# Moving the copy of dt\*x and renaming GpSimd's four input products in a fused attention and state-space kernel

## The chip, the cores and the metric

The kernel runs on one core of a Trainium2 chip. The metric is device microseconds of one execution, as the median of several. Engines are named TensorE (PE), VectorE (DVE), ScalarE (ACT), GpSimd (POOL) and SyncE (SP, which only issues DMAs).

## The reference

Input `x` is (8, 512, 64, 64) in float32: 8 images, 512 channels, 4096 positions. Layer 0 adds a pooled attention; layer 1, which holds nearly all the time, adds this:

```
xn = layer_norm(group_norm(x))                   # over the 512 channels
for each of 4 chunks of 128 channels, per image: # mamba
    xi, z = in_proj(chunk)                       # 256 inner channels each
    xc = silu(causal_conv(xi, 4 taps));  dt, B, C = x_proj(xc)
    dt = softplus(dt_proj(dt) + b)
    for s in range(16):                          # 16 states
        h_s[t] = exp(dt[t] * A_s) * h_s[t-1] + (dt*xc)[t] * B_s[t]
        y[t]  += h_s[t] * C_s[t]
    y = (y + xc * D) * silu(z);  chunk_out = out_proj(y) + skip * chunk
x = x + proj(layer_norm(all chunk_outs))
```

## The kernel before, in words

An image has 8 tiles of 512 positions, a tile has 4 items (the chunks), so there are 8 x 8 x 4 = 256 items. An item holds 256 inner channels as 128 partitions x 2 halves x 512 positions, and is worked off in 16 steps, one for each state s. Here "first" to "fourth item" of a tile are those with `j` = 0, 1, 2, 3 in the code. Each step does the following for its state:

- the **input product** U_s = (dt\*x) \* B_s, 1024 elements per partition. `make_u` stands both on VectorE (L1119) and on GpSimd (L1440); `POOL_U` (L43) names the four states that GpSimd makes, VectorE makes the other twelve. VectorE reads dt\*x from PSUM (`DTP`), GpSimd reads it from SBUF (`DTX`), and B_s is in SBUF;
- the **decay** exp(dt \* A_s) by ScalarE into PSUM (`DA`, `step`, L770), half by half. There is one buffer for each half, so that the decay of step s+1 waits for the scan of the same half of step s;
- the **scan** h_s, two instructions of VectorE (`scan`, L1140), one for each half;
- the **output product** G_s = h_s \* C_s on GpSimd (`out_state`, L1452);
- the **sum** of G_s into PSUM (`YP`) by TensorE with a unit matrix (`state_sum`, L390), issued two steps later in TensorE's order.

U, H and G are rings of 4 slots: the scan of state n waits for the output product n-4, an input product n waits for the scan n-4, and an output product n for the sum n-4.

All engines run their instructions in the order that the code writes, and the front of the next item is interleaved with the steps of this one. Where it stands in the steps (plus one step later in the fourth item, `d` = 1 from `late`, L202):

- TensorE: xi of the next item, first half, at step 15 of the item before (in the third item's case at step 0 of the fourth), second half (`xi_second`) at step 0 + d, ahead of the state sum 15 of the finished item, which is at step 1 (for d = 1 the order is sum 14, xi first half, sum 15, xi second half); z at step 2 + d.
- ScalarE: `xi_copy` at steps 1 + d and 2 + d, the two silus at step 3 + d (they wait for the gate), the softplus of dt at steps 6 to 10. In the fourth item two pieces of `apply_norm` follow the copy of the second half of xi at step 3.
- GpSimd: four products at steps 9 + d to 11 + d that finish dt; the last, `dt_x` (L1478), is dt\*x of the next item. Here its end is called **X** of the next item.
- VectorE: the **gate** (`gate`, L1154) of the finished item after the scan of step 2 + d. It waits for the state sum 15 of that item.
- `dtx_copy` (L843) on ScalarE copies dt\*x from SBUF into PSUM, since VectorE's input products read it there. In the kernel before it stands at step 13 + d of the item before, behind the decay of that step and ahead of the decay of the next; it waits for `dt_x` and for all of VectorE's input products of the item whose dt\*x it overwrites.

The tables `AHEAD` and `AHEAD_LATE` (L47, L48; the second for d = 1) say which input products VectorE issues ahead of the scan of each step; 16 is state 0 of the next item. GpSimd issues its input product of step n+3 ahead of the output product of step n (`U_LEAD`).

SyncE broadcasts two rows of B or of C by one DMA, in the order of the steps.

Of the kernel before, what the change touches and what calls it, by code (L numbers as in the profile page):

```python
# [22 lines left out]
NS = 16  # L23
# [16 lines left out]
B_ROWS = 8  # L40
C_ROWS = 4
SLICE_COLS = T // SS
POOL_U = (1, 7, 8, 10)  # L43
NP_U = len(POOL_U)
ND_U = NS - NP_U
U_LEAD = 3
AHEAD = ((2,), (3,), (), (4,), (5, 6,), (), (), (9,), (), (11,), (12,), (13,), (14,), (15,), (), (16,))  # L47
AHEAD_LATE = ((2,), (3,), (), (4,), (5,), (6,), (), (9,), (), (11,), (12,), (13,), (14,), (15,), (), (16,))  # L48


def block_ssm_kernel(nc, x, wqkv, bq, bk, bv, norm_g, norm_b, w_in, conv_w, conv_b, w_x, w_dt, dt_b,
                     a_log, d_param, w_out, w_proj, proj_b, skip, eye, group_mean, out):
    with ExitStack() as ctx:  # L53
# [128 lines left out]
        def pool_u(n):  # L182

            return n // NS * NP_U + sum(1 for s in POOL_U if s <= n % NS)

# [583 lines left out]
        def _(act):  # L769
# [73 lines left out]
            def dtx_copy(tile, i, first=False):  # L843
                act.wait_ge(dtx_ready, tile * ITEMS + i + 1)
                if not first:
                    act.wait_ge(u_dve, tile * (ND_U * ITEMS) + ND_U * i)
                act.activation(DTP[:, :, :], DTX[:, :, :], ACT.Copy).then_inc(dtx_copied, 1)  # L847
# [36 lines left out]
            def window(tile, w, first=False, front=True, ln1=True, ln2=True, new=False, shifted=False, coming=None, kept=True,  # L884
                       kept_before=True):
                j = w % ITEMS
                d = late(j, new)
                ahead = tile + w // ITEMS
                for s in range(NS):
                    step(tile, w * NS + s, first=first, kept=kept if s else kept_before)  # L890
                    if front:
                        if s == 1 + d:
                            xi_copy(tile, w + 1, 0)
                        if s == 2 + d:
                            xi_copy(tile, w + 1, 1)
                        if s == 3 + d:
                            if not first:
                                act.wait_ge(yz_ready, tile * ITEMS + w)
                            silus(tile, w + 1)
                        if s == 5 + d:  # L900
                            rows_copy(tile, w + 1)
                        if s == 6 + d:
                            dt_split(tile, w + 1, 0)
                        if s == 7 + d:
                            dt_split(tile, w + 1, 1)
                            dt_exp(tile, w + 1)
                        if s == 8 + d:
                            dt_excess(tile, w + 1)
                            dt_log(tile, w + 1)
                        if s == 9 + d:  # L910
                            dt_large(tile, w + 1)
                            dt_small(tile, w + 1)
                        if s == 10 + d:
                            dt_square(tile, w + 1, first=first)
                        if s == 12:
                            if j == 0 and ln2:
                                act.wait_ge(cen2_ready, ahead)
                            skip_term(tile, w + 1)
                        if s == 13 + d:
                            dtx_copy(tile, w + 1)  # L920
                    if j == 0 and ln2 and s == 11:
                        square(cen2_ready, sq2_ready, ahead)
                    if j == 0 and ln2 and s == 15:
                        rstd(RS[:, :], var2_ready, log2_ready, rstd2_ready, ahead)
                    if j == 2 and ln1:
                        if s == 4 + d:
                            act.wait_ge(x1_ready, ahead + 2)
                            if new:
                                act.wait_ge(gshift_ready, coming * 2 + 2)
                            group_norm((0, 1))  # L930
                        if s == 5 + d:
                            group_norm((2, 3), last=True)
                        if s == 9 + d:
                            square(cen1_ready, sq1_ready, ahead + 2)
                        if s == 13 + d:
                            rstd(LP[:, :], var1_ready, log1_ready, rstd1_ready, ahead + 2)
                        if s == 15 and not new:
                            keep_halo()
                            apply_norm(ahead + 2, (0,))
                    if j == 3 and ln1:  # L940
                        if s == 0:
                            if shifted:
                                keep_halo(new=True)
                                apply_norm(ahead + 2, (0,))
                            apply_norm(ahead + 2, (1,))
                        if s == 3:
                            apply_norm(ahead + 2, (2, 3))

                    if coming is not None:
                        if j == 1:  # L950
                            if s == 0:
                                prob_scale(coming)
                            if s == 9:
                                prob_turned(coming)
                            if s == 11:
                                attended(coming, 0)
                            if s == 13:
                                attended(coming, 1)
                        if j == 2 and not new:
                            if s == 14:  # L960
                                group_rstd(coming, 1)
                        if j == 2 and new and s == 1:
                            group_rstd(coming, 2)
                        if j == 3:
                            if s == 2:
                                pooled(coming)
                            if s == 7:
                                summed(coming)
                            if s == 11:
                                head(Q, BQ, q_ps, q_ready, coming, 0)  # L970
                            if s == 12:
                                head(Q, BQ, q_ps, q_ready, coming, 1)
                            if s == 13:
                                head(K, BK, k_ps, k_ready, coming, 0)
                            if s == 15:
                                head(K, BK, k_ps, k_ready, coming, 1)
                        if j == 0:
                            if s == 0:
                                value_copy(coming, 0)
                            if s == 10:  # L980
                                value_copy(coming, 1)
                            if s == 14:
                                prob(coming)
# [134 lines left out]
        def _(dve):  # L1118
            def make_u(tile, n, first=False):  # L1119
                i, s = n // NS, n % NS  # L1120
                if s not in POOL_U:
                    if s == min(set(range(NS)) - set(POOL_U)):
                        dve.wait_ge(dtx_copied, tile * ITEMS + i + 1)
                    if s % 2 == 0 or s - 1 in POOL_U:
                        q = s // 2
                        dve.wait_ge(b_landed[q % (B_ROWS // 2)],
                                    tile * rows_count(ITEMS - 1, NS // 2 - 1, B_ROWS // 2) + rows_count(i, q, B_ROWS // 2))
                    if not (first and n < used(n)):
                        dve.wait_ge(scanned, tile * (2 * STEPS) + 2 * (n - used(n) + 1))
                    dve.tensor_tensor(U[:, slot(n)], DTP[:, :, :], BS[:, s % B_ROWS, :].unsqueeze(1).broadcast_to([P, NH, T]),  # L1130
                                      ALU.mult).then_inc(u_dve, 1)

            def make_ahead(tile, n, d, first=False, front=True):

                s = n % NS
                for m in (AHEAD_LATE if d else AHEAD)[s]:
                    if front or m < NS:
                        make_u(tile, n - s + m, first=first)

            def scan(tile, n, first=False):  # L1140
                i, s = n // NS, n % NS
# [61 lines left out]
            def window(tile, w, stat=None, first=False, front=True, ln1=True, ln2=True, new=False, coming=None):  # L1203

                j = w % ITEMS
                d = late(j, new)
                ahead = tile + w // ITEMS
                for s in range(NS):
                    n = w * NS + s
                    make_ahead(tile, n, d, first=first, front=front)  # L1210
                    scan(tile, n, first=first)
                    if s == 2 + d and not first:
                        gate(tile, w - 1)
# [197 lines left out]

            attention()
            first_front(0, 0)
            make_u(0, 0, first=True)
            window(0, 0, first=True, ln2=False)
            window(0, 1, ln2=False)
            with dve.Fori(0, BATCH - 1) as b:
# [169 lines left out]
```

## Time and profile before

| | |
|---|---|
| median of 3 runs | 16507.46 us (16484.04 to 16516.45) |
| the profiled execution | 16491.02 us, its span 16489.2 us |
| GpSimd busy | 14793.6 us, 90% |
| VectorE busy | 14790.3 us, 90% |
| TensorE busy | 14324.9 us, 87% |
| ScalarE busy | 11509.3 us, 70% |

The span is that of the instructions in the hardware's record; the execution's own time is 1.8 us longer. A busy share is an average over all stages. "Idle before" is time that an engine spent idle in front of an instruction, with the instruction that released it.

### The profile page before, as it was taken

What the parts mean: (1) busy time and instruction counts of PE and PEld (TensorE: products, weight loads), DVE (VectorE), ACT (ScalarE), POOL (GpSimd) and SP (SyncE); (2) the same over time, 40 slices, a digit from 0 to 9 for tenths busy, and PEclk for the clock granted to TensorE, in tenths of its full rate; (3) what the DMA queues carried; (4) which work ended last, traced back from release to release, by engine and by line L of the source; (5) the groups of instructions that cost most, each with busy time, mean ns of one, the idle gap of its engine ahead of it and who ended that gap; (6) DMA issues with size and microseconds to landing.
All of it is one profiled execution on the core that took longest, in us unless ns stands there. A gap on an engine that the chain in (4) does not pass through costs nothing. (4 is left out here: it accounts for less than half of the span.)

```text
span 16489.2 us, 151533 instructions
## 1 busy us (share of the span) xinstructions
PE 14324.9 (87%) x30720; PEld 5799.1 (35%) x30720; DVE 14790.3 (90%) x13024; ACT 11509.3 (70%) x18891; POOL 14793.6 (90%) x6275
## 2 busy tenths in 40 slices
PE   6888989888888888888888888888888888888888
PEld 2333333333333333333333333333333333333333
DVE  6999989999899998999899998999989999888888
ACT  5777767677677667776677776777767677677776
POOL 5999989999899888999899998999989999899998
PEclk9999999999999999999999999999999999999999
DMA  3444444444444444444444444444444444444444
GB/s 131 155 156 157 157 149 158 155 157 154 152 154 156 158 152 155 155 156 163 147 155 156 157 162 147 155 159 157 159 145 158 159 154 160 147 154 157 152 150 136
DMA packets 739078, 2537.58 MB, mean 154 GB/s; under 512 B 77240, under 2 KB 78016, under 8 KB 721728
## 3 DMA queue, kind: packets, MB, share of 16 engines
q1 hardware_dynamic: 738112, 2527.45, 45.7%
q8 instruction: 270, 4.42, 0.1%
q14 instruction: 696, 5.70, 0.1%
HBM read 2376.15 MB, written 150.99 MB: 153 GB/s over the span
## 5 line engine op out<-in xcount | busy, mean ns | idle before, releaser
L1151 DVE TENSOR_TENSOR_SCAN RING<-DA,HS,RING 128x512 f32<-128x512 f32 x8192 | 9944.3, 1263 | 1154.8 <-ACT DA L777 1152.2
L1462 POOL TENSOR_TENSOR RING<-RING,CS 128x1024 f32<-128x1024 f32 x4096 | 9614.3, 2363 | 1443.8 <-DVE RING L1151 1329.1
L388 PE MATMUL YP<-RING,EYE 128*128 128x512 f32 x16384 | 8230.8, 637 | 1603.3 <-POOL RING L1462 1262.9
L777 ACT ACTIVATE DA<-ITEM,AN 128x512 f32<-128x512 f32 x8192 | 5498.6, 684 | 2993.1 <-DVE RING L1151 2974.8
L388 PEld LDWEIGHTS YP<-RING,EYE 128*128 128x128 f32 x16384 | 3169.6, 200 | 6213.3 <-issue 4035.6
L1130 DVE TENSOR_TENSOR RING<-DTP,BS 128x1024 f32<-128x1024 f32 x3072 | 3682.4, 1204 | 303.7 <-ACT DTP L847 295.9
L1449 POOL TENSOR_TENSOR RING<-ITEM,BS 128x1024 f32<-128x1024 f32 x1024 | 2419.9, 2363 | 0.1
L388 PE MATMUL FL<-XN,WC 128*128 128x512 f32 x4096 | 1922.0, 613 | 9.7 <-ACT XN L866 4.6
L388 PEld LDWEIGHTS FL<-XN,WC 128*128 128x128 f32 x4096 | 823.5, 201 | 1084.8 <-issue 1075.5
L847 ACT ACTIVATE DTP<-ITEM 128x1024 f32<-128x1024 f32 x256 | 263.1, 1028 | 1180.2 <-POOL ITEM L1480 1177.6
L388 PE MATMUL FL<-LS,WP 128*128 128x512 f32 x2048 | 987.6, 606 | 42.7 <-DVE XR L1181 36.6
L1467 POOL TENSOR_TENSOR ITEM<-ITEM,EX 128x1024 f32<-128x1024 f32 x256 | 606.3, 2368 | 169.2 <-ACT EX L832 169.2
L787 ACT ACTIVATE HS<-RING 128x2 f32<-128x2 f32 x3648 | 694.4, 190 | 1.5 <-DVE RING L1151 1.5
L388 PE MATMUL FL<-ROWS,WDT 8*128 8x512 f32 x1024 | 583.7, 650 | 109.8 <-ACT ROWS L804 53.6
L388 PE MATMUL FL<-LS,MEAN 128*128 128x512 f32 x1024 | 546.9, 661 | 128.6 <-ACT LS L876 128.6
L1476 POOL TENSOR_TENSOR ITEM<-ITEM,YZ 128x1024 f32<-128x1024 f32 x256 | 601.3, 2349 | 38.7 <-POOL YZ L1471 3.0
L1471 POOL TENSOR_TENSOR YZ<-YZ,EM 128x1024 f32<-128x1024 f32 x256 | 606.2, 2368 | 0.0
L1480 POOL TENSOR_TENSOR ITEM<-ITEM 128x1024 f32<-128x1024 f32 x256 | 600.8, 2347 | 0.1
L388 PEld LDWEIGHTS FL<-LS,WP 128*128 128x128 f32 x2048 | 388.8, 193 | 564.3 <-issue 521.9
L388 PE MATMUL FL<-XN,WZ 128*128 128x512 f32 x1024 | 511.4, 622 | 60.4 <-ACT ITEM L791 60.4
L388 PE MATMUL FL<-YZ,WO 128*128 128x512 f32 x1024 | 507.7, 618 | 1.3 <-DVE YZ L1157 1.3
L388 PE MATMUL FL<-ITEM,WX 128*40 128x512 f32 x1024 | 489.0, 600 | 1.4 <-ACT ITEM L797 1.4
(125 smaller groups left out, 10763.6 us busy)
## 6 DMA issues: line engine op xcount, KB each, us to landing
BS<-bc_rows SPq DMA_DIRECT2D x2048, 512.0 KB, 4.9
CS<-bc_rows SPq DMA_DIRECT2D x2048, 512.0 KB, 3.6
XR<-in_x SPq DMA_DIRECT2D x128, 1024.0 KB, 7.5
x_slices<-XR SPq DMA_DIRECT2D x64, 1024.0 KB, 8.3
XR<-x_slices SPq DMA_DIRECT2D x64, 1024.0 KB, 7.7
out<-XR SPq DMA_DIRECT2D x64, 1024.0 KB, 8.5
XR<-in_wqkv SPq DMA_DIRECT2D x24, 1024.0 KB, 7.8
bc_rows<-ROWS SPq DMA_DIRECT2D x256, 64.0 KB, 4.6
```

The lines of the kernel that those rows point to most:

```text
L388: return pe.matmul(*a, **k)
L777: act.activation(DA[:, h, :], DT[:, i % 2, h, :], ACT.Exp, scale=AN[:, h, s:s + 1]).then_inc(dA_ready, 1)
L787: act.activation(HS[:, i % ITEMS, :, s:s + 1], src, ACT.Copy).then_inc(state_kept, 1)
L847: act.activation(DTP[:, :, :], DTX[:, :, :], ACT.Copy).then_inc(dtx_copied, 1)
L1130: dve.tensor_tensor(U[:, slot(n)], DTP[:, :, :], BS[:, s % B_ROWS, :].unsqueeze(1).broadcast_to([P, NH, T]), ALU.mult).then_inc(u_dve, 1)
L1151: dve.tensor_tensor_scan(H[:, slot(n), h, :], DA[:, h, :], U[:, slot(n), h, :], HS[:, i % ITEMS, h, s:s + 1], ALU.mult, ALU.add).then_inc( ...
L1449: pool.tensor_tensor(U[:, slot(n)], DTX[:, :, :], BS[:, s % B_ROWS, :].unsqueeze(1).broadcast_to([P, NH, T]), ALU.mult).then_inc(u_pool, 1)
L1462: pool.tensor_tensor(G[:, slot(n)], H[:, slot(n)], CS[:, s % C_ROWS, :].unsqueeze(1).broadcast_to([P, NH, T]), ALU.mult).then_inc(g_ready, 1)
L1467: pool.tensor_tensor(DT[:, i % 2], DT[:, i % 2], EX[:, :, :], ALU.add).then_inc(dt_begun, 1)
L1471: pool.tensor_tensor(YZ[:, :, :], YZ[:, :, :], EM[:, :, :], ALU.mult).then_inc(poly_ready, 1)
L1476: pool.tensor_tensor(DT[:, i % 2], DT[:, i % 2], YZ[:, :, :], ALU.add).then_inc(dt_ready, 1)
L1480: pool.tensor_tensor(DTX[:, :, :], DT[:, i % 2], XC[:, i % 2], ALU.mult).then_inc(dtx_ready, 1)
```

## The change

ScalarE's copy of dt\*x moves from step 13 + d of the item before to step 0 of its own item, behind that step's two decays. GpSimd's four input products become those of states 0, 1, 7 and 9, where they were those of 1, 7, 8 and 10. So GpSimd makes U_0 at step 13 of the item before, ahead of G_13, U_1 at step 14 as before, U_7 at step 4 as before and U_9 at step 6; VectorE makes U_8 ahead of scan 6 and U_10 ahead of scan 8, and no U_0, U_7, U_9 (it makes U_2 ahead of scan 1, where it was ahead of scan 0). The counts, four and twelve an item, stay.

```diff
-POOL_U = (1, 7, 8, 10)
+POOL_U = (0, 1, 7, 9)
-AHEAD = ((2,), (3,), (), (4,), (5, 6,), (), (), (9,), (), (11,), (12,), (13,), (14,), (15,), (), (16,))
-AHEAD_LATE = ((2,), (3,), (), (4,), (5,), (6,), (), (9,), (), (11,), (12,), (13,), (14,), (15,), (), (16,))
+AHEAD = ((), (2,), (3,), (4,), (5, 6,), (), (8,), (), (10,), (11,), (12,), (13,), (14,), (15,), (), ())
+AHEAD_LATE = ((), (2,), (3,), (4,), (5,), (6,), (8,), (), (10,), (11,), (12,), (13,), (14,), (15,), (), ())
...
-                        if s == 13 + d:
-                            dtx_copy(tile, w + 1)
+                    if s == 0 and not first:
+                        dtx_copy(tile, w)
...
-            make_u(0, 0, first=True)
             window(0, 0, first=True, ln2=False)
```

The rest of the diff removes the argument `front` of `make_ahead`, which no entry needs any more.

## Rows read from the trace of the kernel before

**Rows 1.** Busy time by engine, and three groups of the page: busy, mean ns, idle before and its releaser.

```profile
PE 14324.9 (87%) x30720; PEld 5799.1 (35%) x30720; DVE 14790.3 (90%) x13024; ACT 11509.3 (70%) x18891; POOL 14793.6 (90%) x6275
...
L1130 DVE TENSOR_TENSOR RING<-DTP,BS 128x1024 f32<-128x1024 f32 x3072 | 3682.4, 1204 | 303.7 <-ACT DTP L847 295.9
L1449 POOL TENSOR_TENSOR RING<-ITEM,BS 128x1024 f32<-128x1024 f32 x1024 | 2419.9, 2363 | 0.1
...
L847 ACT ACTIVATE DTP<-ITEM 128x1024 f32<-128x1024 f32 x256 | 263.1, 1028 | 1180.2 <-POOL ITEM L1480 1177.6
```

**Rows 2.** Windows view of one tile: length, busy PE, PEld, DVE, ACT, POOL; clock, DMA share, GB/s.

```profile
5012.40:5068.60 56.20, 51.86 (x114) 20.49 (x112) 53.00 (x45) 41.85 (x67) 53.37 (x24) 0.98 0.46 158
5068.60:5129.80 61.20, 58.60 (x129) 24.29 (x130) 55.22 (x49) 42.83 (x71) 60.16 (x26) 0.97 0.41 139
5129.80:5192.70 62.90, 55.70 (x119) 22.28 (x118) 56.07 (x48) 46.10 (x74) 59.36 (x27) 0.94 0.53 168
5192.70:5264.30 71.60, 56.63 (x105) 21.42 (x104) 63.82 (x56) 47.55 (x79) 58.23 (x26) 0.81 0.48 157
```

**Rows 3.** GpSimd's timeline of the same tile: start, us, engine, line, operands, count, idle before.

```profile
5010.10 2.34 POOL L1480 TENSOR_TENSOR ITEM<-ITEM 128x1024 f32<-128x1024 f32 x1
5012.40 2.36 POOL L1462 TENSOR_TENSOR RING<-RING,CS 128x1024 f32<-128x1024 f32 x1
5014.71 2.36 POOL L1449 TENSOR_TENSOR RING<-ITEM,BS 128x1024 f32<-128x1024 f32 x1
5017.01 7.00 POOL L1462 TENSOR_TENSOR RING<-RING,CS 128x1024 f32<-128x1024 f32 x3
...
5056.92 2.35 POOL L1462 TENSOR_TENSOR RING<-RING,CS 128x1024 f32<-128x1024 f32 x1
```

**Rows 4.** TensorE's timeline at the start of the tile's first item.

```profile
5017.44 3.99 PE L388 MATMUL YP<-RING,EYE 128*128 128x512 f32 x8
5021.26 3.60 PE L388 MATMUL FL<-XN,WC 128*128 128x512 f32 x8
5024.70 1.88 PE L388 MATMUL YP<-RING,EYE 128*128 128x512 f32 x4
```

**Rows 5.** VectorE's timeline of the same tile.

```profile
5013.76 1.23 DVE L1130 TENSOR_TENSOR RING<-DTP,BS 128x1024 f32<-128x1024 f32 x1 [3.47 <-ACT DTP L847]
...
5026.61 1.22 DVE L1157 TENSOR_TENSOR YZ<-ITEM,YP 128x1024 f32<-128x1024 f32 x1
...
5054.10 2.45 DVE L1151 TENSOR_TENSOR_SCAN RING<-DA,HS,RING 128x512 f32<-128x512 f32 x2
...
5086.77 1.22 DVE L1157 TENSOR_TENSOR YZ<-ITEM,YP 128x1024 f32<-128x1024 f32 x1 [1.06 <-PE YP L388]
...
5147.46 1.20 DVE L1157 TENSOR_TENSOR YZ<-ITEM,YP 128x1024 f32<-128x1024 f32 x1
...
5160.12 2.46 DVE L1151 TENSOR_TENSOR_SCAN RING<-DA,HS,RING 128x512 f32<-128x512 f32 x2 [1.01 <-ACT DA L777]
...
5195.73 2.46 DVE L1151 TENSOR_TENSOR_SCAN RING<-DA,HS,RING 128x512 f32<-128x512 f32 x2 [5.59 <-ACT DA L777]
...
5216.58 1.19 DVE L1157 TENSOR_TENSOR YZ<-ITEM,YP 128x1024 f32<-128x1024 f32 x1
...
5226.94 4.81 DVE L1151 TENSOR_TENSOR_SCAN RING<-DA,HS,RING 128x512 f32<-128x512 f32 x4 [2.18 <-ACT DA L777]
...
5239.77 2.46 DVE L1151 TENSOR_TENSOR_SCAN RING<-DA,HS,RING 128x512 f32<-128x512 f32 x2 [0.48 <-ACT DA L777]
```

**Rows 6.** ScalarE's timeline inside the tile's fourth item.

```profile
5213.94 0.67 ACT L791 ACTIVATE ITEM<-FL,COL 128x512 f32<-128x512 f32 x1
5214.51 1.51 ACT L866 ACTIVATE XN<-LV,COL 128x512 f32<-128x512 f32 x2
5215.92 1.47 ACT L777 ACTIVATE DA<-ITEM,AN 128x512 f32<-128x512 f32 x2
...
5223.88 1.02 ACT L797 ACTIVATE ITEM<-FL 128x1024 f32<-128x1024 f32 x1 [3.99 <-PE FL L388]
```

More of the change, by code:

```diff
@@ L1131, in make_u, with make_ahead @@
                                       ALU.mult).then_inc(u_dve, 1)
-            def make_ahead(tile, n, d, first=False, front=True):
+            def make_ahead(tile, n, d, first=False):
                 s = n % NS
                 for m in (AHEAD_LATE if d else AHEAD)[s]:
-                    if front or m < NS:
-                        make_u(tile, n - s + m, first=first)
+                    make_u(tile, n - s + m, first=first)
             def scan(tile, n, first=False):
@@ L1209, in window @@
                     n = w * NS + s
-                    make_ahead(tile, n, d, first=first, front=front)
+                    make_ahead(tile, n, d, first=first)
                     scan(tile, n, first=first)
```

## The prediction

> **What bounds the kernel now.** I read the busy shares first, then the windows of one tile, then the engines' timelines inside it. The shares show no single bound: VectorE and GpSimd are both busy 90%, and both idle about a tenth [rows 1]. The reader should also see who waits for dt\*x: ScalarE's copy stands idle 1180.2 us in front of it, 4.6 us an item, and VectorE's input products 295.9 us behind the copy [rows 1]. By windows, the four items of a tile last 56.2, 61.2, 62.9 and 71.6 us, and GpSimd is busy 53.4, 60.2, 59.4 and 58.2 us of them: the second item is GpSimd's, the fourth is nobody's, with 7.8 us idle on VectorE and 13.4 on GpSimd [rows 2]. The timeline of VectorE shows the stall that the copy makes: 3.47 us at the start of the first item, 5.59 at that of the fourth (there as a wait for a decay that is queued behind the copy) [rows 5].
>
> What must be seen next is that another chain runs beside that stall. X is the end of dt\*x (5012.4, 5068.6, 5129.8, 5192.7, the edges of the windows). In the first item GpSimd then makes G_13, U_1, G_14, G_15, one every 2.31 us [rows 3]; G_14 ends at X + 6.9 = 5019.3. TensorE sums 13 and 14 until 5021.4, makes half of xi in 3.6 us, then sum 15, which ends at 5026.6 [rows 4], and the gate starts at 5026.61 [rows 5]. So the gate of the first item is already set by GpSimd and TensorE, 7.3 us after G_14, and the stall in front of VectorE's scans is fully covered by it. The second item's gate waits 1.06 us for TensorE as well; the third's and fourth's have no wait in front of them [rows 5], there VectorE is the later one.
>
> **The change, part by part.** I write every cost as what it shifts in X-to-X of an item, since dt\*x of one item leads to that of the next.
>
> *The copy moved.* The stall goes on ScalarE and VectorE. In its new place the copy costs ScalarE 1.03 us [rows 1] behind the decays of step 0; VectorE wants it for U_2 after scan 0. Scan 0 now can't start before U_0, at X + 2.3 in the first item and X + 4.6 in the others (below), and takes 2.45 us: more than the copy. Cost 0, from 0 to 1.0 us an item if the cover is gone.
>
> *U_0 on GpSimd, ahead of G_13.* GpSimd's sum is unchanged, four input products as before. U_0 needs row 0 of B two steps earlier than VectorE did; it comes by the DMA that brings U_1's row, and GpSimd's input products idled 0.1 us in all in front of them [rows 1], so 0, and at most the 2.31 us between U_0 and the old place of U_1 if the row comes only then. But between X and G_14 there is one more product, 2.31 us [rows 3]. In the first item dt\*x comes after G_12, so G_14 ends at X + 4 x 2.31 = 9.2 and the gate starts at X + 9.2 + 7.3 = 16.5, where it was 5026.6 - 5012.4 = 14.2: +2.3 us. In the other three G_12 is still to come: G_14 ends at X + 5 x 2.31 = 11.6, the gate is at X + 18.9. That is 5087.5 for 5086.8 in the second (+0.7), 5148.7 for 5147.5 in the third (+1.2), 5211.6 for 5216.6 in the fourth (-5.0) [rows 5]. VectorE is no longer late there: scan 0 at X + 4.6, U_2, scan 1 at X + 9.2 (behind U_1), U_3, scan 2 ends at X + 15.2; the fourth item has U_4 and scan 3 too and ends at X + 18.8, just in time. What is late next is named by that: where VectorE waited for the copy, it waits for the gate.
>
> *What the fourth item's earlier gate is worth.* Not 5.0 us. TensorE issues there sum 14, xi, sum 15, xi: by the pitches of rows 4 about 10.7 us behind G_14 (5192.7 + 11.6 = 5204.3), so 5215.0. ScalarE copies that half (0.67 us), applies two norms and only then makes the decay of step 4: 5217.1, where it was 5215.92. From this decay to scan 5 it is 5226.94 - 5215.92 = 11.0 us, of which 3.99 were a wait for z, which goes with the early gate [rows 6]: 7.0. Scan 5 starts at 5224.1, 2.8 us earlier than in rows 5. With nothing in the way it would be 5.0, with the norms in the way once more it would be 1.4; I take 2.8.
>
> *U_8 and U_10 on VectorE, U_7 and U_9 on GpSimd.* VectorE's sum stays 12. But between the gate and scan 10, whose end releases the last four of GpSimd's products ahead of dt\*x, it had U_4, 5, 6, 9, 11, 12 and now has U_4, 5, 6, 8, 10, 11, 12 (the fourth item one less in both): +1.2 us [rows 1], from 0 if a wait swallows it to 1.2. In the third item U_8 stands where VectorE waited 1.01 us for a decay, and in the fourth behind it one of 0.48 [rows 5]: 0.2 and 0.7 net. GpSimd's U_7 and U_9 are both done some 5 us before their scans: 0.
>
> *The sum for a tile.* First item: 2.3 + 1.2 - 0.4 (scan 10 ended near 5056.5 [rows 5], G_10 started at 5056.9 [rows 3]) = +3.1. Second: 0.7 + 1.2 lie under a GpSimd that is busy 60.2 of 61.2 us and whose work doesn't shrink [rows 2]: 0, from -1.0 to +1. Third: 1.2 + 0.2 = +1.4. Fourth: -2.8 + 0.7 = -2.1. Together +2.4 us; for 64 tiles +154 us. I take off a tenth for the 14 tiles that carry the next image's attention and have waits of their own: +140 us. The profiled execution took 16491.0 us, 16 us under the median shown; on the median 16507 + 140 gives 16647, and I say 16645 us.
>
> **A rule weighed.** Rows 1 put VectorE and GpSimd level at 90%, and rows 5 show a gap that returns every item. The Trainium skill (Perfetto Trace Analysis, Optimization Strategy) says to take the most occupied engine, find the gaps on it and make what they wait for come sooner. By that rule closing this gap pays; the first rival below prices it from rows. Rows 4 and 5 speak against it in the first two items, where the gate doesn't wait for VectorE.
>
> **The rivals.**
> *The gap is given back.* The mechanism is that VectorE's lateness runs through to dt\*x in every item. The end is where the item meets GpSimd's busy time: 56.2 - 53.4 = 2.8, 1.0, 3.5 us, and 5.6 in the fourth [rows 2, 5], 12.9 us a tile, 826 us in all, 15.68 ms. For it speaks the 7.8 us of idle VectorE in the fourth item, against it that sum 15 ended exactly where the gate began. Chance 0.07.
> *The fourth item gives all.* The second half of xi doesn't hold ScalarE up, scan 5 comes 5.0 us earlier: 3.1 + 0 + 1.4 - 4.3 = +0.2 us a tile, 13 us, within what can be told from no change (0.2%, 33 us). Chance 0.18. If in addition VectorE's added product disappears in waits in the first, third and fourth items (-1.2, -0.2, -0.7), it is -1.9 a tile, -120 us, 16.39 ms, faster; it decides against my forecast once the fourth item gains over 4.5 us and the product costs nothing. Chance 0.16.
> *The fourth item gives nothing.* Scan 3 ends only 0.1 us ahead of the new gate; if the item start is later (the norm's scaling and scan 15 stand right before it on VectorE), 3.1 + 1.4 + 0.7 = +5.2 us a tile, +333 us, 16.84 ms. Chance 0.08.
>
> **How the numbers follow.** My forecast has 0.51, with its own range 16560 to 16760 (0.9 to 4 us a tile). Faster by over 0.2%: 0.07 + 0.16, and a little of the rest, 0.24. Within 0.2%: 0.18. Slower: 0.58. The range for 8 in 10 leaves out the first rival and half of its neighbour below, and the upper part of the last: 16390 to 16840.
>
> **What would show it.** In the profile after: the first item of a tile lasts 59 us (56.2), the fourth 69 to 70 (71.6), the second unchanged. The idle in front of the copy is near 0, and idle of VectorE in front of the gate (released by TensorE) rises from 1 to above 3 us in the first three items. Scan 5 of the fourth item still waits for a decay. It is wrong if the gate comes under 16 us after X in the first item, if the fourth item drops by 4 us or more, or if scan 10 follows the gate by no more than before (29.9 us to its end).

## The result, and the profile after

The changed kernel takes 16732.33 us (median of 4, 16730.29 to 16744.97) against 16510.03 us before: 1.0139 times as long, 95% interval 1.0122 to 1.0157. That is +222 us where +138 were forecast. The profiled execution took 16744.97 us, the slowest of its four, and the one before the change (16491.02 us) lay under its median: the two traces differ by 254 us in their spans, some 31 us more than the medians, and all sums over traces below are out of these 254.

The page of the changed kernel, with the lines that answer to [rows 1] (L1447 is GpSimd's input product, L1150 the scan, L1156 the gate):

```profile
PE 14423.7 (86%) x30720; PEld 5830.5 (35%) x30720; DVE 14874.7 (89%) x13024; ACT 11534.6 (69%) x18891; POOL 14784.6 (88%) x6275
...
L1150 DVE TENSOR_TENSOR_SCAN RING<-DA,HS,RING 128x512 f32<-128x512 f32 x8192 | 9978.3, 1266 | 1033.8 <-POOL RING L1447 569.9
...
L1130 DVE TENSOR_TENSOR RING<-DTP,BS 128x1024 f32<-128x1024 f32 x3072 | 3682.7, 1204 | 4.6 <-issue 3.3
L1447 POOL TENSOR_TENSOR RING<-ITEM,BS 128x1024 f32<-128x1024 f32 x1024 | 2416.0, 2359 | 9.4
...
L1156 DVE TENSOR_TENSOR YZ<-ITEM,YP 128x1024 f32<-128x1024 f32 x256 | 310.8, 1214 | 664.3 <-PE YP L388 664.3
```

The stall is gone: VectorE's input products idle 4.6 us where it was 303.7, and ScalarE's copy 11.6 where it was 1180.2. Yet the span is longer, while GpSimd's total busy time is the same to 0.1% and VectorE's is up by 0.6%. In front of the gate VectorE now idles 664.3 us, released by TensorE's sums; before the change it was 63.6. A second wait is new: of the scans' 1033.8 us of idle time, 569.9 are waits for GpSimd's input products (e_late01 below bears on it).

The windows view of one tile, whose columns are those of [rows 2], cut at X as there:

```profile
5341.50:5400.70 59.20, 54.15 (x114) 21.38 (x112) 52.30 (x46) 41.48 (x67) 53.46 (x24) 0.94 0.44 149
5400.70:5461.80 61.10, 56.95 (x126) 23.67 (x127) 54.97 (x49) 42.78 (x71) 60.18 (x27) 0.97 0.41 140
5461.80:5524.40 62.60, 55.19 (x123) 22.31 (x122) 57.28 (x50) 48.17 (x77) 59.33 (x27) 0.98 0.51 170
5524.40:5595.00 70.60, 56.69 (x105) 21.09 (x104) 64.01 (x57) 46.27 (x77) 58.02 (x25) 0.81 0.46 159
```

Against [rows 2] the first item is 3.0 us longer (59.2), the second and third are within 0.3 us (61.1, 62.6), the fourth is 1.0 shorter. GpSimd's busy time is the same in each.

GpSimd's timeline at the start of the first item, X = 5341.6:

```profile
5341.67 2.35 POOL L1447 TENSOR_TENSOR RING<-ITEM,BS 128x1024 f32<-128x1024 f32 x1
5343.97 2.35 POOL L1460 TENSOR_TENSOR RING<-RING,CS 128x1024 f32<-128x1024 f32 x1
5346.28 2.37 POOL L1447 TENSOR_TENSOR RING<-ITEM,BS 128x1024 f32<-128x1024 f32 x1
5348.60 11.61 POOL L1460 TENSOR_TENSOR RING<-RING,CS 128x1024 f32<-128x1024 f32 x5
```

The rows are U_0, G_13, U_1 and then G_14 and four more. G_14 ends at 5350.9, X + 9.3, where it ended at X + 6.9 [rows 3]. VectorE's timeline of the same tile:

```profile
5344.30 2.46 DVE L1150 TENSOR_TENSOR_SCAN RING<-DA,HS,RING 128x512 f32<-128x512 f32 x2 [2.54 <-POOL RING L1447]
...
5358.17 1.22 DVE L1156 TENSOR_TENSOR YZ<-ITEM,YP 128x1024 f32<-128x1024 f32 x1 [3.31 <-PE YP L388]
...
5386.48 2.45 DVE L1150 TENSOR_TENSOR_SCAN RING<-DA,HS,RING 128x512 f32<-128x512 f32 x2
...
5419.57 1.22 DVE L1156 TENSOR_TENSOR YZ<-ITEM,YP 128x1024 f32<-128x1024 f32 x1 [3.32 <-PE YP L388]
...
5480.62 1.22 DVE L1156 TENSOR_TENSOR YZ<-ITEM,YP 128x1024 f32<-128x1024 f32 x1 [3.31 <-PE YP L388]
...
5544.46 2.46 DVE L1150 TENSOR_TENSOR_SCAN RING<-DA,HS,RING 128x512 f32<-128x512 f32 x2 [3.51 <-ACT DA L777]
5546.84 1.20 DVE L1156 TENSOR_TENSOR YZ<-ITEM,YP 128x1024 f32<-128x1024 f32 x1
...
5557.04 2.46 DVE L1150 TENSOR_TENSOR_SCAN RING<-DA,HS,RING 128x512 f32<-128x512 f32 x2 [2.02 <-ACT DA L777]
```

Scan 0 waits 2.54 us for U_0 (L1447), and the gate of the first item starts at 5358.17, X + 16.6, after 3.31 us of waiting for TensorE. This is a tile with a short first item; over all of them the gate is at one of two places (see below). In the second and third item it starts at 5419.57 and 5480.62, X + 18.8 in both. Scan 10 of the first item (5386.48) ends 30.8 us behind the start of the gate, where it was 29.9.

### The profile page after: what moved, and what is told of

It is laid out like the page before. It is cut to its first block and busy times, and to the rows that moved or that the text cites. A ratio compares the mean times of both kernels' runs of the same rounds, so it can differ in the third digit from the quotient of the medians.

```text
span 16742.8 us, 151165 instructions
## 1 busy us (share of the span) xinstructions
PE 14423.7 (86%) x30720; PEld 5830.5 (35%) x30720; DVE 14874.7 (89%) x13024; ACT 11534.6 (69%) x18891; POOL 14784.6 (88%) x6275
## 5 line engine op out<-in xcount | busy, mean ns | idle before, releaser
L1150 DVE TENSOR_TENSOR_SCAN RING<-DA,HS,RING 128x512 f32<-128x512 f32 x8192 | 9978.3, 1266 | 1033.8 <-POOL RING L1447 569.9
L388 PE MATMUL YP<-RING,EYE 128*128 128x512 f32 x16384 | 8387.0, 645 | 1634.8 <-POOL RING L1460 1579.9
L1447 POOL TENSOR_TENSOR RING<-ITEM,BS 128x1024 f32<-128x1024 f32 x1024 | 2416.0, 2359 | 9.4
L791 ACT ACTIVATE ITEM<-FL,COL 128x512 f32<-128x512 f32 x512 | 350.0, 684 | 1459.9 <-PE FL L388 1459.1
L1156 DVE TENSOR_TENSOR YZ<-ITEM,YP 128x1024 f32<-128x1024 f32 x256 | 310.8, 1214 | 664.3 <-PE YP L388 664.3
```

The lines of the kernel that those rows point to most:

```text
L388: return pe.matmul(*a, **k)
L791: act.activation(XC[:, i % 2, h, :], FL[:, h, :], ACT.Identity, bias=CB[:, h:h + 1]).then_inc(xi_copied, 1)
L1150: dve.tensor_tensor_scan(H[:, slot(n), h, :], DA[:, h, :], U[:, slot(n), h, :], HS[:, i % ITEMS, h, s:s + 1], ALU.mult, ALU.add).then_inc( ...
L1447: pool.tensor_tensor(U[:, slot(n)], DTX[:, :, :], BS[:, s % B_ROWS, :].unsqueeze(1).broadcast_to([P, NH, T]), ALU.mult).then_inc(u_pool, 1)
```

## The experiments

All ratios are to the kernel before, timed on the same chip. The diffs are against the changed kernel unless another is named; `AHEAD_LATE` is changed like `AHEAD` and left out. Item lengths are means over the ordinary tiles (six of the eight of an image, without the last image and the very first tile), from the ends of all 256 products dt\*x; before the change they are 56.3, 61.6, 62.4 and 71.4 us, after it 60.1, 61.7, 63.0 and 70.7.

**e_sets: the new sets, the copy in its old place.**

```diff
-                    if s == 0 and not first:
-                        dtx_copy(tile, w)
+                    if front and s == 13 + d:
+                        dtx_copy(tile, w + 1)
```

> The changed kernel's sets and tables with the copy back at step 13 + d of the item before. My theory (the gate is set by G_14 and by TensorE behind it; one product of GpSimd more ahead of G_14 and one of VectorE more between the gate and scan 10 cost the time; the stall at the copy is covered): about as slow as the changed kernel, first item 59 to 61 us, gate at X + 16.5 to 18, ratio to before 1.013 to 1.020. Rival (the copy's new place costs the time): no slower than before, 0.995 to 1.003.

Measured: 1.0131 (1.0114 to 1.0148), 16722.22 us; items 60.1, 61.7, 62.7, 70.5. It is as slow as the changed kernel. Its VectorE timeline at the start of a first item (X = 5077.2), only the instructions with idle time before them:

```profile
5079.00 4.81 DVE L1150 TENSOR_TENSOR_SCAN RING<-DA,HS,RING 128x512 f32<-128x512 f32 x4 [3.92 <-ACT DA L777]
...
5095.55 1.22 DVE L1156 TENSOR_TENSOR YZ<-ITEM,YP 128x1024 f32<-128x1024 f32 x1 [4.77 <-PE YP L388]
```

The stall of the copy is there in full (3.92 us), and the gate behind it (X + 18.4 in this tile, one with a slow sum, see below) waits another 4.77 us for TensorE. So with these sets the stall lies beside a longer wait and costs nothing, and the copy's new place gains nothing. The rival, that the new place costs the time, is out.

**e_copy: the sets of before, the copy later.**

```diff
-POOL_U = (0, 1, 7, 9)
+POOL_U = (1, 7, 8, 10)
-AHEAD = ((), (2,), (3,), (4,), (5, 6,), (), (8,), (), (10,), (11,), (12,), (13,), (14,), (15,), (), ())
+AHEAD = ((0, 2,), (3,), (), (4,), (5, 6,), (), (), (9,), (), (11,), (12,), (13,), (14,), (15,), (), ())
-                    if s == 0 and not first:
-                        dtx_copy(tile, w)
+                    if front and s == 15:
+                        dtx_copy(tile, w + 1)
```

> The sets of before (1, 7, 8, 10), with the copy at step 15 of the item before, behind that step's decays, and U_0 by VectorE ahead of scan 0 of its own item. G_14 stays where it was before and no product is added behind the gate; only the stall goes. My theory: first and second item unchanged (56.2, 61.2), third -1.0, fourth -3 to -4 us; ratio 0.980 to 0.988. Rival 1 (the stall is covered everywhere): 0.997 to 1.003. Rival 2 (the gap is given back in every item): 0.95 to 0.965.

Measured: 0.9744 (0.9728 to 0.9761), 16087.15 us; items 56.3, 60.7, 61.2, 66.0. That is below my range and above that of rival 2: the fourth item gave 5.3 us and not 3 to 4, and the second 0.9 where I had none. The windows of one tile:

```profile
5139.60:5196.30 56.70, 54.10 (x114) 21.45 (x112) 52.64 (x46) 42.36 (x68) 53.33 (x25) 0.94 0.44 158
5196.30:5256.50 60.20, 57.03 (x129) 23.61 (x130) 56.50 (x51) 43.59 (x74) 60.06 (x26) 1.00 0.40 140
5256.50:5318.30 61.80, 55.35 (x119) 22.33 (x118) 55.60 (x49) 47.04 (x77) 59.32 (x27) 0.94 0.51 173
5318.30:5383.80 65.50, 54.65 (x105) 20.29 (x104) 63.31 (x56) 45.43 (x76) 58.10 (x26) 0.86 0.47 171
```

The first item is as long as before, to 0.5 us, though its stall went; the second is at GpSimd's 60.1; most of the gain is in the fourth. The gates of this tile and scan 5 of the fourth item:

```profile
5154.23 1.22 DVE L1156 TENSOR_TENSOR YZ<-ITEM,YP 128x1024 f32<-128x1024 f32 x1 [2.72 <-PE YP L388]
...
5212.78 1.22 DVE L1156 TENSOR_TENSOR YZ<-ITEM,YP 128x1024 f32<-128x1024 f32 x1 [3.04 <-PE YP L388]
...
5273.00 1.22 DVE L1156 TENSOR_TENSOR YZ<-ITEM,YP 128x1024 f32<-128x1024 f32 x1 [3.77 <-PE YP L388]
...
5336.71 1.19 DVE L1156 TENSOR_TENSOR YZ<-ITEM,YP 128x1024 f32<-128x1024 f32 x1
...
5346.91 4.81 DVE L1150 TENSOR_TENSOR_SCAN RING<-DA,HS,RING 128x512 f32<-128x512 f32 x4 [2.02 <-ACT DA L777]
```

From X they start at 14.5, 16.5, 16.5 and 18.4 us in this tile (in most second items at 18.1, which costs nothing, since GpSimd bounds them), where the changed kernel has 16.6, 18.8, 18.8 and 22.5. Scan 5 of the fourth item starts at X + 28.6, where it was X + 34.3 [rows 5] and is X + 32.7 after the change. So closing the stall is worth 2.6% with the old sets and nothing with the new ones. Against the kernel before two things have moved in this run, both to close the stall: ScalarE's copy, and VectorE's U_0, from ahead of scan 15 to ahead of the next scan 0. They were not tried one by one, and the copy stands at step 15 here and at step 0 in the changed kernel.

**e_bonly: U_1 on VectorE, U_2 on GpSimd.**

```diff
-POOL_U = (0, 1, 7, 9)
+POOL_U = (0, 2, 7, 9)
-AHEAD = ((), (2,), (3,), (4,), ...
+AHEAD = ((), (1,), (3,), (4,), ...
```

> The changed kernel with the set (0, 2, 7, 9): VectorE makes U_1 ahead of scan 1, GpSimd U_2 behind G_14. So one product less stands ahead of G_14 (the gate of the first item back at X + 14.2), but VectorE still makes seven input products between the gate and scan 10. My theory: first item 57 us, second 61.0, third -0.8, fourth -3 us against before; ratio 0.984 to 0.992. Rival (the product behind the gate is the whole cost): as slow as the changed kernel, 1.010 to 1.015.

Measured: 0.9890 (0.9874 to 0.9907), 16326.95 us; items 57.0, 61.0, 62.3, 67.3. One product less of GpSimd ahead of G_14, with VectorE's products behind the gate unchanged, takes off 2.5% from the changed kernel, 3.1 us of it in the first item and 3.4 in the fourth.

**e_late01: and six input products between gate and scan 10.**

```diff
-POOL_U = (0, 1, 7, 9)
+POOL_U = (0, 7, 8, 10)
-AHEAD = ((), (2,), (3,), (4,), (5, 6,), (), (8,), (), (10,), (11,), ...
+AHEAD = ((), (1, 2,), (3,), (4,), (5, 6,), (), (), (9,), (), (11,), ...
```

> The changed kernel with the set (0, 7, 8, 10): VectorE makes U_1 and U_2 ahead of scan 1, and six input products between gate and scan 10, as before. Neither of the two costs of my theory is left: first item 56.2, second 61.0, third -1.0, fourth -3.5 us against before; ratio 0.980 to 0.988, below the set (0, 2, 7, 9) by 0.003 to 0.006. Rival (the copy at step 0 is late): 1.00 or over.

Measured: 0.9745 (0.9728 to 0.9761), 16088.02 us; items 56.4, 60.8, 61.3, 65.9. The step from e_bonly is thus worth 1.45%, more than the 0.6% at most that I expected of it: 0.6 us in the first, 1.0 in the third and 1.4 in the fourth item. It is not the one product between gate and scan 10 alone, for GpSimd's U_2 also goes from ahead of G_15. In the first item that changes nothing (the gate stands at X + 14.3 in both), in the third and fourth it brings the gate 0.3 us nearer to X at the median; the rest lies behind the gate. The copy at step 0 isn't late: this equals e_copy, where it stands one step earlier. Nor is the scans' new wait for GpSimd the cost: U_0 is GpSimd's here too, the scans still wait 391.3 us for its input products, and the gain is in full.

**e_norm: the changed kernel with the fourth item's two norms later.**

```diff
-                        if s == 3:
+                        if s == 5:
                             apply_norm(ahead + 2, (2, 3))
```

> The changed kernel with the two norms of the fourth item moved from step 3 to step 5 of ScalarE. In the changed kernel's trace the decay of step 4 starts behind them and scan 5 at X + 32.7. My theory (ScalarE's own order, not VectorE, holds the fourth item after the gate): scan 5 comes about 1.4 us earlier, fourth item 69.3 for 70.7, others the same, ratio to before 1.009 to 1.011 (the changed kernel 1.014). Rival (the fourth item is held by the gate alone, or by VectorE): 1.013 to 1.015.

Measured: 1.0074 (1.0060 to 1.0088), 16636.80 us; items 59.6, 61.9, 63.1, 69.2. The fourth item shortens by 1.5 us where 1.4 were expected; the ratio is a little under my range. VectorE's scan 5 and ScalarE's norms in one fourth item, X = 5228.8:

```profile
5251.20 1.20 DVE L1156 TENSOR_TENSOR YZ<-ITEM,YP 128x1024 f32<-128x1024 f32 x1
...
5259.99 2.46 DVE L1150 TENSOR_TENSOR_SCAN RING<-DA,HS,RING 128x512 f32<-128x512 f32 x2 [0.61 <-ACT DA L777]
```

```profile
5260.60 1.50 ACT L866 ACTIVATE XN<-LV,COL 128x512 f32<-128x512 f32 x2
```

Scan 5 starts at X + 31.2, where the changed kernel has 32.7. The part of the ratio beyond that is in the first items (last section).

**e_copy_norm: the same on e_copy.** Its diff is the two above together.

> The kernel with only the copy moved (ratio 0.974) and the two norms at step 5. Same theory, same 1.4 us: fourth item 64.6 for 66.0, ratio 0.969 to 0.972. If VectorE is by now the later one there: 0.974.

Measured: 0.9708 (0.9693 to 0.9723), 16037.72 us; fourth item 65.0, 1.0 us shorter.

**e_u4: no input product of GpSimd ahead of G_14.**

```diff
-POOL_U = (1, 7, 8, 10)
+POOL_U = (4, 7, 8, 10)
-AHEAD = ((0, 2,), (3,), (), (4,), (5, 6,), (), (), (9,), (), (11,), ...
+AHEAD = ((0,), (1, 2,), (3,), (), (5, 6,), (), (), (9,), (), (11,), ...
```

(against e_copy, with the copy at step 15)

> Copy at step 15 of the item before, GpSimd's set (4, 7, 8, 10): neither U_0 nor U_1 nor any other input product of GpSimd between X and G_14; VectorE makes U_0, U_1, U_2 ahead of scans 0 and 1, and five input products between gate and scan 10. My theory: G_14 comes 2.31 us earlier after X than in the kernel before and the stretch behind the gate is 1.2 us shorter: first item 54 us (from 56.3, then GpSimd's own 53.4 is near), second 60.5, third 60.5, fourth 64; ratio 0.955 to 0.965. Rival (GpSimd waits for the rows of B or for scan 0 in front of U_4, and the gain stops): 0.970 to 0.978.

Measured: 0.9634 (0.9619 to 0.9648), 15907.26 us; items 55.2, 60.4, 60.0, 65.6. It beats both kernels, but not by the way I expected. One tile:

```profile
4825.30:4880.40 55.10, 51.59 (x114) 20.60 (x112) 52.52 (x46) 42.25 (x68) 53.41 (x24) 0.98 0.47 162
4880.40:4940.80 60.40, 56.91 (x130) 23.80 (x131) 58.05 (x52) 44.15 (x74) 60.15 (x26) 1.00 0.41 140
4940.80:5000.20 59.40, 53.42 (x119) 21.60 (x118) 54.35 (x47) 46.64 (x74) 59.26 (x26) 0.98 0.53 179
5000.20:5066.70 66.50, 52.62 (x105) 19.92 (x104) 64.11 (x57) 45.75 (x76) 58.17 (x26) 0.91 0.49 169
```

In the second and third item GpSimd is busy 60.15 of 60.40 and 59.26 of 59.40 us: in this tile these can't shorten any more. The fourth is nearly as long as in e_copy (65.6 for 66.0), with VectorE at 64.1 of 66.5. The first was to be 54 us and is 55.2. TensorE's rows show why:

```profile
4823.05 3.78 PE L388 MATMUL YP<-RING,EYE 128*128 128x512 f32 x4 [3.33 <-POOL RING L1460]
4826.63 3.99 PE L388 MATMUL FL<-XN,WC 128*128 128x512 f32 x8
4830.46 3.60 PE L388 MATMUL YP<-RING,EYE 128*128 128x512 f32 x8
```

G_14 ends at X + 4.6, 2.3 us earlier than before the change, but the gate starts only 0.2 us earlier (X + 13.9 for 14.2, medians of 48 first items). From sum 12 on, which starts ahead of X, TensorE has no idle time: sum 12, half of xi, sums 13 and 14, half of xi, sum 15. With the product gone from ahead of G_14 it is TensorE's own queue that sets the gate, and the first item's gain of 1.1 us lies nearly all behind it. Before the change the two were level there: sum 14 waited at most 0.4 us for G_14.

**e_u4_norm: and the two norms later.**

> Copy at step 15, GpSimd's set (4, 7, 8, 10), and the two norms at step 5. If ScalarE's order still holds the fourth item behind an earlier gate, it is 64.2 for 65.6 us and the ratio 0.958 to 0.961 (0.963 without the norms' move); if VectorE or GpSimd holds it by now, 0.963. The second item can't shorten: it is at GpSimd's own 60.2.

Measured: 0.9632 (0.9619 to 0.9645), 15915.36 us: nothing gained, fourth item 65.7. ScalarE's timeline in e_u4's fourth item shows why:

```profile
5018.43 1.51 ACT L866 ACTIVATE XN<-LV,COL 128x512 f32<-128x512 f32 x2
...
5026.12 1.02 ACT L797 ACTIVATE ITEM<-FL 128x1024 f32<-128x1024 f32 x1 [2.50 <-PE FL L388]
```

Behind the norms ScalarE waits 2.50 us for z from TensorE anyway, so what they take is covered. In the changed kernel's fourth item, whose start is shown in the next section, ScalarE has no idle time in front of its read of z.

## Why the prediction came out as it did

The direction and the mechanism were right, and the cost was forecast too small: +138 us for +222. The terms of the sum that were mis-sized are the fourth item's gain and the tiles with attention work; the third item's term erred the other way and hid a part of it, which is luck.

*The gate is set by G_14 and TensorE, not by the copy's stall.* Right. The second's and third's gate was forecast at X + 18.9 and stands at 18.8. The first's was forecast at X + 16.5; it stands at 16.6 in 19 of 48 ordinary first items and 1.6 us later in the other 29. e_sets shows the stall covered with the new sets, e_copy with the old ones in the first item, e_bonly that the product ahead of G_14 is the larger cost.

*First item +3.1.* In the tile shown it is +3.0; the mean over 57 first items is +3.7 (the seven last ones of an image, which carry attention work, have +0.5). Of the 48 in seven tiles of seven images (without the very first) 29 last about 60.9 us and 19 about 59.2. In all 29 the sum 14 takes over 3 us, in none of the 19. TensorE's rows of one long and one short first item, and the windows of these very sums with the granted clock third from the end:

```profile
5095.91 3.58 PE L388 MATMUL YP<-RING,EYE 128*128 128x512 f32 x4 [2.25 <-POOL RING L1460]
```

```profile
5351.00 1.98 PE L388 MATMUL YP<-RING,EYE 128*128 128x512 f32 x4 [1.80 <-POOL RING L1460]
```

```profile
5095.90:5099.50 3.60, 3.59 (x5) 1.68 (x6) 3.60 (x4) 0.82 (x2) 3.60 (x2) 0.55 0.08 17
```

```profile
5351.00:5353.00 2.00, 2.00 (x5) 1.04 (x6) 2.00 (x3) 0.82 (x2) 2.00 (x1) 1.00 0.02 6
```

The sum takes 3.58 us with 0.55 of the clock granted, so nearly all of it at the lower of the two levels (1.2 GHz), and 1.98 at the full one (2.4 GHz). TensorE had idled 2.25 us in front of the one and 1.80 in front of the other. This sum is on the path now, 1.6 us each time. In none of the 48 before the change did it take over 2 us: there sum 13 and 14 ran back to back behind xi [rows 4]. The forecast used the duration of [rows 4] for a sum that now follows a wait.

*Second item 0.* Right for 50 of 64 (within 0.1 us on average) and mis-sized for the 14 in which VectorE also computes the next image's statistics, +2.3 us on average, 32 us in all. Nine of these grew by 3.5 us; two were already 68.0 us before the change and shrank by 2.6. That VectorE bounds them and not GpSimd, so that both costs show, is how I read them; no run was made for them. I had read the second item from one tile in which there are none.

*Third item +1.4.* The gate came as forecast; the item is +0.6. Before the change these items were of two lengths, near 61.3 and near 62.9, the longer with slow matmuls in front of a wait of VectorE for the channel mean, and I had taken a long one; after it they are at 62.6. The wait in one of the long ones before the change:

```profile
3125.81 2.29 DVE L1167 TENSOR_TENSOR LV<-LV,FL 128x2048 f32<-128x2048 f32 x1 [1.43 <-PE FL L388]
```

*Fourth item -2.1.* This is the term that was mis-sized most, -0.7 us on average. I let the gate move from X + 23.9 to X + 18.9 and scan 5 by 2.8 us. In the changed kernel VectorE waits 3.51 us for the decay of step 3 and the gate starts at X + 22.5, behind scan 3. ScalarE's timeline there:

```profile
5543.16 0.69 ACT L791 ACTIVATE ITEM<-FL,COL 128x512 f32<-128x512 f32 x1 [5.95 <-PE FL L388]
5543.75 1.29 ACT L777 ACTIVATE DA<-ITEM,AN 128x512 f32<-128x512 f32 x2
...
5548.31 0.69 ACT L791 ACTIVATE ITEM<-FL,COL 128x512 f32<-128x512 f32 x1 [3.15 <-PE FL L388]
5548.90 1.51 ACT L866 ACTIVATE XN<-LV,COL 128x512 f32<-128x512 f32 x2
5550.31 1.29 ACT L777 ACTIVATE DA<-ITEM,AN 128x512 f32<-128x512 f32 x2
```

ScalarE stands at step 2 in front of the copy of xi's first half, 5.95 us, and the decay of step 3 is queued behind it. Xi's first half comes behind sum 14, hence behind G_14. I had followed ScalarE's queue from the second half of xi on and not from the first, and so had the gate too early. But that error is not what the item lost: ScalarE waits again, 3.15 us, for the second half, and only then come the norms, the decay of step 4 at 5550.31 (X + 25.9, forecast X + 24.4) and scan 5 (X + 32.7, forecast X + 31.4). What is late there is TensorE, and it is sum 14 again:

```profile
5535.98 3.71 PE L388 MATMUL YP<-RING,EYE 128*128 128x512 f32 x4 [2.10 <-POOL RING L1460]
...
5544.68 3.60 PE L388 MATMUL FL<-XN,WC 128*128 128x512 f32 x8
```

The second half of xi ends 12.3 us behind G_14, where I had 10.7 from the pitches of [rows 4]. One fourth item of e_norm (X = 3425.7) shows what the slow sum costs, for there alone among its ordinary ones the sum took 1.98 us (2.4 to 3.8 in the others, where xi behind it takes up the rest):

```profile
3437.32 1.98 PE L388 MATMUL YP<-RING,EYE 128*128 128x512 f32 x4 [2.64 <-POOL RING L1460]
```

```profile
3446.45 1.20 DVE L1156 TENSOR_TENSOR YZ<-ITEM,YP 128x1024 f32<-128x1024 f32 x1
```

The item is 67.5 us long, where the others are 69.2, and its gate is at X + 20.7, where theirs is at 22.4. So 1.7 us of the fourth item are TensorE's slow stretch at sum 14, about as much as the term was off by (1.4), and the gate would have been 1.8 us later than forecast even with a fast one. e_norm confirms what stands behind: take the norms out of that queue and scan 5 moves by about the 1.4 us that the forecast gave them.

*One product between gate and scan 10, +1.2.* Right in kind: +0.9 from the gate to the end of scan 10 in the tile shown, and e_bonly against e_late01 gives 0.6, 1.0 and 1.4 us in the first, third and fourth item (with the reserve said there).

The sum: the items before and after differ by 214 us in the first, 30 in the second, 46 in the third and -34 in the fourth, together 256 us in the profiled executions; forecast were 198, 0, 90 and -134, less a tenth. The tenth was taken off for the 14 tiles with attention work, and it had the wrong sign: they make 70 us of the difference where the forecast had about 20. Nearly all is in the seventh tile of seven images, 11 us each (4.6, 3.4, 3.5 and -0.6 in its four items). Of the rivals, "the fourth item gives nothing" came nearest in time (16.84 ms against 16.73), and the late gate it names is there, though through ScalarE and not through VectorE; but the fourth item did gain, and what it missed came from TensorE. "The gap is given back" fell for this change and would have been half right for the copy alone, which gives 422 us where 826 were the most. For the rule of the Trainium skill (Perfetto Trace Analysis, Optimization Strategy) the runs show both outcomes: closing the gap paid 2.6% with the old sets (e_copy), and nothing with the new ones, which made a second chain longer (e_sets against the changed kernel).

## What to carry to other kernels

Where engines feed each other in a ring, follow one turn from event to event and price each edit by what it adds between two events of that turn; busy totals that stay equal (here GpSimd's, to 0.1%) say nothing. A stall that is taken away pays only as far as the next chain into the same wait is shorter, so don't pay for its removal with work on that chain: e_copy gets 2.6% where the change, with the same stall removed, loses 1.4%. A gain on that chain in turn pays only as far as the next one: with no product ahead of G_14 (e_u4) the gate came 0.2 us earlier and not 2.3. And a duration read where an engine runs back to back need not hold where the same instruction follows a wait: here 1.98 us became 3.6, and it is what the forecast's terms for the first and the fourth item lacked.

## What was not expected of the hardware

A sum of the same four records took 1.98 or 3.58 us, with the clock granted during it at 1.00 or 0.55. Before the change the sum was fast in all 48 first items, with at most 0.4 us of idle time in front of it; after it, it decides 1.6 us of an item, and the same program meets it in some tiles and not in others (a long first item in 29 of 48 in the changed kernel, 23 in e_sets, 8 in e_norm, which changes nothing in the first item itself). From 29 to 8 at 1.7 us each is 36 us; a part is lost again in the last image, and all 64 first items of e_norm together are 26 us shorter than the changed kernel's, 0.16%, about the part of its ratio beyond the fourth item. The idle time of TensorE just before this sum was 1.9 to 2.3 us in the 29 and either 1.6 to 1.8 or 2.6 in the 19, so a longer wait alone doesn't make it slow. Why TensorE is at the lower level in one tile and not in the next was not tried.

In the third item of the seventh tile VectorE copies 4 elements per partition. Before the change that took 1.6 us in each of seven images, after it 4.5; a like copy in the tile that follows takes under 0.2:

```profile
3878.25 1.56 DVE L1272 COPY SM<-SM 128x4 f32<-128x4 f32 x1
```

```profile
3936.88 4.54 DVE L1271 COPY SM<-SM 128x4 f32<-128x4 f32 x1
```

In all 14 it ends 24 to 30 ns behind the end of an instruction of GpSimd, so it reads like a wait for that engine, which no run tested. It makes 3.0 of that item's 3.5 us, 21 us in all, and no term of the forecast had it.
